# Where the second weights of the experts are loaded and split: order of the loads, and who makes the low halves

## The reference

```python
x = x + 0.5 * ffn(layernorm(x), ...)
x = x + attention(layernorm(x), context, Wq, Wk, Wv, Wout, bout)
x = x + 0.5 * ffn(layernorm(x), ...)

def ffn(x, gate_w, gate_b, expert_bias, w1, b1, w2, b2):      # 8 experts, 128 -> 512 -> 128
    top_idx = argmax(x @ gate_w.T + gate_b + expert_bias)
    for e in range(8):
        y = relu(x @ w1[e] + b1[e]) @ w2[e] + b2[e]
        out = out + where(top_idx == e, y, 0)
```

## Time and profile before

| | |
|---|---|
| time, median of 3 runs | 751.51 us (751.04 to 751.72) |
| the profiled execution's own time | 751.08 us |
| its span, first to last instruction | 749.3 us |
| granted TensorE clock, mean | 0.990 |
| busy in the span: PE, DVE, ACT, POOL | 711.1, 603.0, 496.9, 363.2 us |
| tiles of the first expert layer | from about 43 to 148 us |

### The profile page before, as it was taken

How to read it: one execution, slowest core, us unless ns; L and a number is a source line. 1 busy time by engine, 2 the same in 40 slices (tenths; PEclk the granted TensorE clock), 3 DMA queues, 4 the chain that set the end, 5 groups by cost and what they waited for, 6 DMA issues and landing times.

```text
span 749.3 us, 15246 instructions
## 1 busy us (share of the span) xinstructions
PE 711.1 (95%) x4374; PEld 595.9 (80%) x4374; DVE 603.0 (80%) x1648; ACT 496.9 (66%) x1212; POOL 363.2 (48%) x496
## 2 busy tenths in 40 slices
PE   8979899999999999999999999999999999989992
PEld 7758797778888888878878888887887887769991
DVE  6979898887787878878788787788878787788882
ACT  3676677678677677667667767766766775546660
POOL 5056787343334445346345444544634633576662
PEclk9999999999999999999999999999999999999996
DMA  9932342200000000000000000000000011232210
GB/s 249 339 143 42 93 85 74 63 19 1 1 1 1 1 5 12 1 2 14 1 1 12 5 2 8 8 0 1 16 1 1 16 43 57 100 87 63 58 47 5
DMA packets 31792, 31.49 MB, mean 42 GB/s; under 512 B 5049, under 2 KB 26183, under 8 KB 31200
## 3 DMA queue, kind: packets, MB, share of 16 engines
q1 hardware_dynamic: 27360, 23.91, 10.7%
q0 software_dynamic: 3520, 6.40, 3.3%
q10 hardware_dynamic: 832, 0.21, 0.1%
HBM read 20.96 MB, written 10.47 MB: 42 GB/s over the span
## 4 chain that ended last, share of the span: by engine, by line
PE 75%; DVE 13%; issue 3%; DMA 3%; POOL 2%; ACT 1%; another core or an unknown queue 0%; DVEq 0%; POOLq 0%; SPq 0%; ACTq 0%
PE bank L1449 16%; PE bank L1451 15%; PE bank L1450 15%; PE bank L1660 13%; PE bank L1496 5%; PE bank L1484 3%; DVE neg_max L1334 2%; DVE probsT_lo L1340 2%; PE bank L1499 2%; DVE hT_lo L1192 1%; DMA rows<-in_L_attn_x 1%; POOL rows L561 1%; PE bank L1506 1%; DVE h L1171 1%; PE bank L1592 1%
## 5 line engine op out<-in xcount | busy, mean ns | idle before, releaser
L577 POOL TENSOR_SCALAR probs<-probs,row_inv 128x512 f32<-128x512 f32 x256 | 177.8, 695 | 274.2 <-DVE row_inv L1345 263.4
L786 ACT ACTIVATE probs<-bank,neg_max 128x512 f32<-128x512 f32 x256 | 176.1, 688 | 144.3 <-DVE neg_max L1334 143.2
L1334 DVE TENSOR_REDUCE neg_max<-bank 128x1 f32<-128x512 f32 x256 | 176.5, 690 | 86.7 <-PE bank L1451 83.4
L1340 DVE TENSOR_TENSOR probsT_lo<-bank,probsT_hi 128x512 fp32r<-128x512 f32 x256 | 174.3, 681 | 2.2 <-ACT probsT_hi L795 2.0
L1660 PEld LDWEIGHTS bank<-ident,probs 128*128 128x128 f32 x1024 | 127.2, 140 | 38.4 <-issue 1.7
L1660 PE MATMUL bank<-ident,probs 128*128 128x128 f32 x1024 | 153.4, 272 | 1.7 <-POOL probs L577 1.3
L795 ACT ACTIVATE probsT_hi<-bank 128x512 fp32r<-128x512 f32 x256 | 150.8, 589 | 2.1 <-PE bank L1660 2.1
L1449 PE MATMUL bank<-m_hi,xT_hi 128*128 128x512 f32 x256 | 122.4, 478 | 0.0
L1449 PE MATMUL bank<-probsT_hi,vw_hi 128*128 128x512 f32 x256 | 101.7, 397 | 3.4 <-DVE probsT_lo L1340 3.4
L1450 PE MATMUL bank<-probsT_lo,vw_hi 128*128 128x512 f32 x256 | 101.5, 396 | 0.0
L1451 PE MATMUL bank<-probsT_hi,vw_lo 128*128 128x512 f32 x256 | 101.4, 396 | 0.0
(11 more groups left out here) (220 smaller groups left out, 1237.0 us busy)
## 6 DMA issues: line engine op xcount, KB each, us to landing
b<-in_L_ffn_b SPq DMA_DIRECT2D x4, 1024.0 KB
x_packed<-slot_rows SPq DMA_DIRECT2D x39, 65.5 KB
slot_rows<-slots SPq DMA_DIRECT2D x39, 65.5 KB
x_stats<-rows SPq DMA_DIRECT2D x4, 524.0 KB, 10.0
rows<-x_packed SPq DMA_DIRECT2D x8, 262.0 KB, 2.7
rows<-in_L_attn_x SPq DMA_DIRECT2D x4, 512.0 KB, 8.3
w_lo<-in_L_ffn_w SPq DMA_DIRECT2D x8, 256.0 KB, 7.4
w_hi_lo<-in_L_ffn_w SPq DMA_DIRECT2D x8, 256.0 KB, 5.7
```

The costliest lines, as they stand in the source:

```text
L577: pool.tensor_scalar(PR[:, u % 4, :], PR[:, u % 4, :], RI[:, u % 4:u % 4 + 1], 1.0, ALU.mult, ALU.mult).then_inc(normed, 1)
L786: act.activation(PR[:, n % 4, :], BK[n % 2][:, :], ACT.Exp, bias=NM[:, n % 4:n % 4 + 1], accum_out=SU[:, n % 4:n % 4 + 1]).then_inc(probs, 1)
L1334: v.tensor_reduce(NM[:, n % 4:n % 4 + 1], BK[n % 2][:, :], AX.X, ALU.max, negate=True)\
L1340: v.tensor_tensor(PTL[at], BK[2 + u % 2][:, :].rearrange("p (c q) -> p c q", c=KC), PTH[at].bitcast(fp32), ALU.subtract).then_inc(pT_lo, 1)
```

## The change

The loads: b1's first half goes ahead of W2; W2 has three semaphores, for experts 0 to 2, 3 to 5 and 6 to 7; b2 waits for the landing of the first gather, W2's last two and b1's second half for the landing of the second. W1's eight semaphores become four, for two experts each. The high parts of W2 move from before the tiles and steps 0 and 1 to the norm of tile 0 and steps 0 to 4; the lows of experts 0 to 4 are made by DVE behind the steps' own work in steps 0, 2, 3 and 4, those of 5 to 7 by GpSimd behind its eighth gather and before its first `add_low`. DVE halves b2 in step 1 and makes the packed-row table in step 0. Every expert gets at least one tile, so that tile j has an expert of number j at most; PE therefore waits tile by tile for the lows up to number j.

```diff
-        w1_in, w2_in = [sem(f"w1_in{e}") for e in range(E)], sem("w2_in")
+        W2_PARTS = [range(0, 3), range(3, 6), range(6, E)]
+        w1_in, w2_in = [sem(f"w1_in{k}") for k in range(E // 2)], [sem(f"w2_in{k}") for k in range(len(W2_PARTS))]
...
+        W2_HIGHS = {0: [2], 1: [3, 4], 2: [5], 3: [6], 4: [7]}
+        W2_LOWS = {0: [0, 1], 2: [2], 3: [3], 4: [4]}
+        POOL_LOWS = range(5, E)
...
-            for e in range(E):
-                load_w2(e)
             load_b1(0)
+            load_w2(0)
+            load_w2(1)
+            sp.wait_ge(place_ps, NCH)
+            sp.wait_ge(pool_moved[0], 16)
+            load_b2(0)
+            sp.wait_ge(pool_moved[1], 16)
+            load_w2(2)
             load_b1(1)
-            sp.wait_ge(place_ps, NCH)
-            load_b2(0)
...
+            def w2_low(e):                                     # GpSimd
+                pool.wait_ge(w2_hi, e + 1)
+                apart(pool, pool_passed)
+                pool.tensor_tensor(W2HL[:, e, :, 1, :], W2RAW[:, e, :, :], W2HL[:, e, :, 0, :].bitcast(fp32),
+                                   ALU.subtract).then_inc(w2_lo_pool, 1)
...
                 gather(j + LEAD)
+                if j == 0:
+                    for e in POOL_LOWS:
+                        w2_low(e)
                 add_low(0, j)
...
             def w1_high(e):
-                act.wait_ge(w1_in[e], 16)
+                act.wait_ge(w1_in[e // 2], 16 * 2)
...
             def w2_high(e):
-                act.wait_ge(w2_in, 16 * E)
+                part = [k for k in range(len(W2_PARTS)) if e in W2_PARTS[k]][0]
+                act.wait_ge(w2_in[part], 16 * len(W2_PARTS[part]))
...
-            for e in range(4):
-                w2_high(e)
...
+                    if r == 0 and m == 0:                      # ScalarE, behind slot_norm(m + 1)
+                        w2_high(1)
...
                         head(BEFORE_FFN + m)
-                        w2_high(4 + 2 * m)
-                        w2_high(5 + 2 * m)
+                    if r == 0 and m in W2_HIGHS:
+                        for e in W2_HIGHS[m]:
+                            w2_high(e)
...
                 slot_norm(0)
+                if r == 0:
+                    w2_high(0)
...
-                    link(v.tensor_scalar(CNTI[:, 0, :], total, float(first), None, ALU.add), step, count)
+                    link(v.tensor_scalar(CNTI[:, 0, :], total, float(least), float(first), ALU.max, ALU.add), step, count)
...
-            half_b2()
-            w2_low(0)
-            w2_low(1)
...
-                        dve.wait_ge(b1_in, 32 * (r + 1))
+                        dve.wait_ge(b1_in[0], 16 * (r + 1))
+                    if m == (2 if r else E // 2 + 2):
+                        dve.wait_ge(b1_in[1], 16 * (r + 1))
...
-                    if r == 0 and m < 3:
-                        for e in range(2 + 2 * m, 4 + 2 * m):
+                    if r == 0 and m == 1:
+                        half_b2()
+                    if r == 0 and m in W2_LOWS:
+                        for e in W2_LOWS[m]:
                             w2_low(e)
-                    if r == 0 and m == 3:
+                    if r == 0 and m == 0:
                         packed_rows()
...
-                    if m == 4 and r == 0:
-                        pe.wait_ge(w2_lo, E)
+                    if r == 0 and 4 <= m < 4 + POOL_LOWS[0]:
+                        pe.wait_ge(w2_lo, m - 3)
+                    if r == 0 and m - 4 in POOL_LOWS:
+                        pe.wait_ge(w2_lo_pool, m - 3 - POOL_LOWS[0])
```

More of the change, by code:

```diff
@@ L195, in macaron_kernel @@
         w1_hi, w1_lo, w2_hi, w2_lo = sem("w1_hi"), sem("w1_lo"), sem("w2_hi"), sem("w2_lo")
+        w2_lo_pool = sem("w2_lo_by_pool")
         head_kept, head_hi = sem("m_then_vw_kept"), sem("m_then_vw_hi")
@@ L227, in macaron_kernel @@
         tail_ready, tail_filled = sem("tail_ready"), sem("tail_filled")
-        b1_in = sem("b1_in")
+        b1_in = [sem(f"b1_in{k}") for k in range(2)]
         b2_in = sem("b2_in")
@@ L367, in load_w1, with load_w2 @@
             def load_w1(e):
-                sp.dma_start(W1RAW[:, e, :], w1[e]).then_inc(w1_in[e], 16)
-            def load_w2(e):
-                sp.dma_start(W2RAW[:, e, :, :], w2[e].rearrange("(c p) d -> p c d", p=P)).then_inc(w2_in, 16)
+                sp.dma_start(W1RAW[:, e, :], w1[e]).then_inc(w1_in[e // 2], 16)
+            def load_w2(k):
+                for e in W2_PARTS[k]:
+                    sp.dma_start(W2RAW[:, e, :, :], w2[e].rearrange("(c p) d -> p c d", p=P)).then_inc(w2_in[k], 16)
             def load_b1(k):
                 own = slice(E // 2 * k, E // 2 * (k + 1))
-                sp.dma_start(B1[:, own, :], b1[own].partition_broadcast(P)).then_inc(b1_in, 16)
+                sp.dma_start(B1[:, own, :], b1[own].partition_broadcast(P)).then_inc(b1_in[k], 16)
             def load_b2(r):
@@ L930, in _, with count_tiles @@
             table_count = [[0], [0]]
-            def count_tiles(r, total, first, i):
+            def count_tiles(r, total, first, i, least=0):
                 step, count = table_step[r], table_count[r]
                 if i == 0:
-                    link(v.tensor_scalar(CNTI[:, 0, :], total, float(first), None, ALU.add), step, count)
+                    link(v.tensor_scalar(CNTI[:, 0, :], total, float(least), float(first), ALU.max, ALU.add), step, count)
                 elif i == 1:
@@ L959, in places @@
                 for i in range(3):
-                    count_tiles(0, total0, P - 1, i)
+                    count_tiles(0, total0, P - 1, i, 1)
                 ends_of(0)
```

## The result

In a comparison of 17 runs of each kernel on one chip the changed kernel took 744.59 us (742.71 to 747.90) and the kernel before 748.28 (744.37 to 754.60); the ratio is 0.9939, 95% interval 0.9920 to 0.9957, so **4.6 us less (3.2 to 6.0)**. The forecast was 3.0 us less, at 748.5 (746.2 to 750.6), so the absolute time is missed by 3.9 us. Of these 3.2 lie in the level: 751.51 was the median of only three runs, and in four comparisons the kernel before had medians from 745.77 to 751.96. The other 0.7 is the gain, 3.7 us by the two medians. By the ratio, which is the better measure of the difference, the gain is 1.6 us larger than forecast.

The account below looks back on a forecast made before the run. TensorE in attention, untouched, fills most of the span; only the first expert layer's start counts. Start 5.1 us earlier, less 2.1 for VectorE blocked by GpSimd: 3.0 us off 751.5 gives 748.5 us, range 746.2 to 750.6.

Parts of the forecast that it names:

- Norm 0: ScalarE's norm of tile 0 was to start at 41.53 instead of 43.60, 2.07 us earlier, ahead of the four highs.
- each hidden: Moved loads at the start: b2, W2's last quarter and b1's half land 1.5, 3 and 5 us before they are wanted.
- The meetings: GpSimd's lows 5 to 7 block VectorE's b2 add and lows 3 and 4: 0.9, 0.7, 0.9 us; 2.1 taken.
- the stalls of the first layer behind gathers: Waits such as TensorE's 1.96 us before 85.81 were to move along with the tiles, adding nothing to the sum.
- Its mirror: A first-layer stall behind a gather, as that before 85.81, goes away: 745.5 us, chance 0.04.
- (a): First expert layer: VectorE and GpSimd hinder each other little; gain 4.3 to 5.1 us, 746.4 to 747.2, chance 0.20.
- (b): Start less early: first gather late or clock still low, costing 1.5 to 2.1 us; gain about 1.2, 750.3, chance 0.12.
- (c): Gain given back later: a first-layer stall behind a gather grows or a new one comes; no change, 751.5, chance 0.09.
- (d): W2's last quarter lands late and holds ScalarE: 750.7, or slower than before at 753 or more; chance 0.05.
- (e): Norm of tile 0 was waiting for its gather anyway, so only the moved loads help; chance counted in (b).
- even under the full load: Before the change, the first gather was said to have landed by 43.60 with all early loads still moving.
- the 2.6 us of the prediction: Time from a gather's start to the norm reading it, from tile 15; put the first gather's landing near 40.1.

Follow-up runs that it names:

- the two edits together: Changed kernel with b1's second half behind the landing of gather 5 and the lows of experts 5 to 7 on VectorE: 746.24 us, ratio 0.9934 to the kernel before.
- The third profile of the changed kernel: The changed kernel, nothing edited, run once more beside later experiments: 741.30 us, ratio 0.9945 to the kernel before.
- the second run: Repeat of the changed kernel with all loads issued as before the change: 751.68 us, ratio 0.9991 to the kernel before.

## Why the prediction was right and wrong

**Right, to the tenth.** Norm 0 at 41.51 (41.53), head 6 done at 44.42 (44.5), full clock from 45 to 50, VectorE's low part of tile 2 at 49.01 (49.1).

**Wrong: "each hidden".** I asked when the moved loads themselves land, and they are in time. I did not ask what is queued with them: gathers 2 to 6 go out in the same microseconds. Gather 3 took 8.4 us to its norm (7.6 to 8.9 in the five profiles where b1's half goes out with it and its norm waits). It cost TensorE 2.18 us of idling, and the clock behind it.

**The meetings: right in kind, hidden in place.** With gather 3 late, hT_lo of tile 0 came at 52.03 instead of 50.7 and the meetings fell elsewhere: two b2 adds, 1.0 us together. With the half of b1 out of the way all three came, at 0.79, 0.54 and 1.07 us, together 2.4, for a forecast of 0.9, 0.7 and 0.9. VectorE's instruction lasts to the end of GpSimd's low plus about its own work: the b2 adds end 0.14 to 0.16 us behind it, the two W2 lows 0.55. Both instructions read two inputs from SBUF. The Trainium skill (SBUF — State Buffer, SBUF: two separate sides) has this as a lock for the whole instruction, by which the second one fully blocks, and these rows agree. In the other direction the rows show only little: GpSimd's add of the earlier trace rows, and the low of 53.24, which overlaps VectorE's low of 52.84 to 53.54 and takes 1.43 us instead of 1.28. Because one cover took the other's place, y of tile 3 stood at 60.96 for a forecast of 60.4: nearly right by luck, through a mechanism that I did not have.

**The step that failed in the sum:** "the stalls of the first layer behind gathers go by tile, not by clock time, and should move along". The sum put this term at nothing. The forecast was a gain of 3.0, the profile shows 2.5 at tile 3 and 1.9 more from tile 8 to 17, where the stall before 85.81 was; together 4.3, for the measured 4.6. Its mirror, a stall that goes, had a chance of 0.04 at 745.5. The stall is made by one transfer, the fill, that goes out 0.4 us behind a gather, and moving it away is worth 3.0 us (1.4 to 4.7) in the kernel before. It does not go by tile alone. With the fill behind store 8 and seven gathers ahead, the three profiles with no low on GpSimd (the kernel before and two experiments) have it 0.39 to 0.40 us behind gather 16, and norm 16 waits 2.28 to 3.12 us; the six with lows on GpSimd have it 1.28 to 2.04 behind, and norm 16 waits 0 to 0.87, norm 17 0.64 to 2.10. Why the lows shift it is read, not tried. SP's waits from 60 to 90 us, before and changed (us in total, times, longest):

```profile
SPq L423 <- DMA x_packed<-slot_rows: 12.2, 9, 3.4
SPq L424 <- POOL slot_rows L530: 4.7, 5, 3.1
```

```profile
SPq L438 <- DMA x_packed<-slot_rows: 13.0, 9, 2.6
```

Each store waits for the one before it to land. My reading, which no run tests, is that the lows stand ahead of GpSimd's first add, so the stores start with a backlog; the chain of landings then sets the place of store 8 and of the fill, where before GpSimd's adds set part of it.

**The rivals.** (a) names a gain of 4.3 to 5.1 us, and the measured 4.6 lies there, but not for its reason: the start gained only 2.5, the meetings cost their full price once gather 3 was on time, and the rest comes from the stall. (b) came in a form that I had ruled out: the start was early, and the low clock came back 5 us later. (c) is what the two edits together show: 2.5 us won at tile 3, of which 1.4 are lost by tile 8 to VectorE's lows and 1.1 by tile 17 to the stall. (d) did not happen: ScalarE waited for no load of W2 from 36 to 62 us. (e) as it stands is refuted, since norm 0 did start at 41.51, but it was right in one half: with the loads in their old place norm 0 waits 3.08 us for its gather, and ScalarE's new order gains nothing. My sentence that the first gather landed by 43.60 "even under the full load", taken as a sign that its time is short, hid this: the later loads are the part that the rest of the change needs.

**The level.** Three runs were too few for the absolute number: the other fourteen runs of that comparison go from 744.37 to 754.60 us. 748.28 less 3.0 would have been 745.3, 0.7 from the measured 744.59.

## What to carry to other kernels

When loads are moved behind a small transfer that a step waits for, ask not only whether they land in time but which small transfers are queued next to them in their new place, and put the large ones behind the last that matters. A stall behind a gather that has one large transfer beside it hangs on tenths of a microsecond, so a change ahead of it can switch it on or off: look for that transfer first, and move it, before the rest is judged. Two covers over the same path show nothing when one is taken off; take both. And look at the steps behind the start as well: work given back to an engine whose steps are already as long as TensorE's costs there what it saved before.

## What was not expected of the hardware

A gather of 128 rows was there within 2.5 to 2.8 us of its start at best (2.6 for tile 15 of the kernel before). Where a norm had to wait for one in the steady stretch, away from the fill, it took 2.9 to 4.8 us. Beside the fill of 458 KB it took 4.8 to 6.2 (gather 16 where the fill is 0.4 us behind it, gather 17 where the fill is 1.3 behind gather 16 or more); with 1.6 MB of plain loads issued alongside 7.6 to 8.9; and 7.3 beside the full early load. So the 2.6 us of the prediction was a lower end, not a usual value.

TensorE's granted clock fell from full (2.4 GHz) to half (1.2 GHz) around idle times: in the kernel before to 0.50 from 45 to 48 us, behind 2.36 us of idling; in the changed kernel to 0.50 from 53 to 56, behind 2.18 us; with the loads as before to 0.52 from 44 to 48, within 3.48 us of idling and behind it. The third profile of the changed kernel has the fall behind only 1.34 us. It stayed at 1.00 with the half of b1 moved, where the longest such gap was 1.02 us, but also behind the 1.96 us before 85.81 in the kernel before (1.00 from 85 to 90). So the length of one gap does not decide it. One execution of the loads in their old place shows the fall early. TensorE had idled 0.92 us for x at 9.60 (not the 1.95 that the expectation of the second run names), and the clock was 0.65 from 10 to 12; the stretches behind are (columns as in the earlier trace rows):

```profile
12.00:20.00 8.00, 8.00 (x44) 7.96 (x43) 5.38 (x40) 1.20 (x2) 4.94 (x3) 0.50 1.07 334
20.00:28.00 8.00, 8.00 (x46) 7.71 (x45) 4.45 (x17) 3.33 (x7) 0.00 (x0) 0.50 1.07 353
```

Sixteen microseconds at half clock, in a run of 753.98 us where the kernel's median is 749.61; norm 0 starts at 50.02. In the profiles of the kernel before and of the changed one TensorE has no gap at this place and the same stretches are at 1.00. A transfer late by a microsecond at the start is thus the first thing that differs in that one run, and probably its cause; it was seen once, and that it makes the scatter of 744 to 754 us in all the others was not tried.
